# One state-space block on one core: moving the step-size series, its exponential and the taps within four passes

## What is computed

```python
proj = einsum('bld,pd->blp', hidden_states, in_proj_w)     # gate | x,B,C | dt
conv = conv_bias + sum_k pad[:, k:k+L, :] * conv_weight[:, k]   # 4 taps
xBC = silu(conv)
dt_p = softplus(dt + dt_bias)
dA = exp(dt_p * -exp(A_log))
# scan: state = state * dA + (dt_p * x) outer B ;  y_t = state . C
y = (ys + x * D) ; yn = y * rsqrt(mean(y*y) + EPS) * norm_weight * silu(gate)
out = einsum('bli,di->bld', yn, out_proj_w)
```

## Time and profile before

| | us |
|---|---|
| median of 3 runs (lowest, highest) | 1552.02 (1550.84, 1553.86) |
| the profiled execution, its own time | 1551.53 |
| its span | 1549.7 |
| PE busy | 1522.1 (98%) |
| DVE busy | 1109.2 (72%) |
| ACT busy | 753.7 (49%) |
| POOL busy | 657.8 (42%) |

### The profile page before, as it was taken

The page is one execution under the profiler, slowest core; times in us unless marked ns, Lnnn a source line. Parts: engine busy times, 40 slices in busy tenths (PEclk is TensorE's granted clock), DMA queues, the critical chain, the costliest instruction groups (busy, mean ns, idle before and its releaser), DMA issues. The chain is left out here.

```text
span 1549.7 us, 31996 instructions
## 1 busy us (share of the span) xinstructions
PE 1522.1 (98%) x12855; PEld 1244.9 (80%) x12855; DVE 1109.2 (72%) x1717; ACT 753.7 (49%) x1306; POOL 657.8 (42%) x687
## 2 busy tenths in 40 slices
PE   7999999999999999999999999999999999999997
PEld 6878888888888888888778888888888888888686
DVE  5977777776667767677787767777676767777566
ACT  4754445445454445445465444545454544544452
POOL 3553544435253544434335352535434352533406
PEclk9999999999999999999999999999999999999999
DMA  5220212122120212121014121102121121113212
GB/s 202 79 86 22 69 35 71 53 62 62 49 76 17 74 35 69 55 62 49 18 55 127 55 69 49 57 27 76 42 69 56 55 69 48 52 32 99 94 36 109
DMA packets 57843, 97.71 MB, mean 63 GB/s; under 512 B 9120, under 2 KB 17824, under 8 KB 57696
## 3 DMA queue, kind: packets, MB, share of 16 engines
q1 hardware_dynamic: 57696, 95.67, 20.2%
HBM read 86.73 MB, written 8.91 MB: 62 GB/s over the span
## 5 line engine op out<-in xcount | busy, mean ns | idle before, releaser
L461 PE MATMUL PS<-xh,wh 128*128 128x512 f32 x1280 | 518.7, 405 | 0.6 <-DVE xl L959 0.6
L1027 DVE SCALAR_TENSOR_TENSOR cb<-PS,P,cb 128x496 f32<-128x496 f32 (+2 forms) x576 | 412.5, 716 | 129.5 <-ACT cb L768 115.9
L461 PE MATMUL PS<-xh,wl 128*128 128x512 f32 x1280 | 501.1, 391 | 0.0
L461 PE MATMUL PS<-xl,wh 128*128 128x512 f32 x1280 | 500.4, 391 | 0.0
L1321 POOL TENSOR_TENSOR wl<-rw,wh 128x512 fp32r<-128x512 f32 x160 | 209.9, 1317 | 214.6 <-ACT wh L714 214.4
L1331 POOL TENSOR_TENSOR ysum<-yq 128x256 f32<-128x256 f32 x128 | 109.2, 853 | 442.3 <-ACT yq L808 441.9
L461 PEld LDWEIGHTS PS<-xh,wl 128*128 128x128 f32 x1280 | 240.5, 188 | 52.5
L461 PEld LDWEIGHTS PS<-xh,wh 128*128 128x128 f32 x1280 | 240.9, 188 | 51.3 <-issue 1.0
L461 PEld LDWEIGHTS PS<-xl,wh 128*128 128x128 f32 x1280 | 241.1, 188 | 45.3
L768 ACT ACTIVATE cb<-PS,P 128x512 f32<-128x512 f32 x192 | 148.3, 772 | 195.4 <-PE PS L461 195.4
L557 PE MATMUL PS<-oh,yh 128*128 128x512 f32 x512 | 200.7, 392 | 4.9 <-issue 3.3
(11 more groups left out here) (188 smaller groups left out, 1880.7 us busy)
## 6 DMA issues: line engine op xcount, KB each, us to landing
rw<-in_w_in SPq DMA_DIRECT2D x160, 256.0 KB, 2.8
ro<-in_w_out SPq DMA_DIRECT2D x64, 256.0 KB, 2.9
dab<-rates SPq DMA_DIRECT2D x128, 128.0 KB, 3.1
x2s<-acc SPq DMA_DIRECT2D x16, 256.0 KB, 3.1
out_x<-acc SPq DMA_DIRECT2D x16, 256.0 KB, 3.0
acc<-in_x SPq DMA_DIRECT2D x3, 1024.0 KB, 9.8
wh<-x2s SPq DMA_DIRECT2D x8, 256.0 KB, 3.8
wl<-x2s SPq DMA_DIRECT2D x8, 256.0 KB, 4.5
```

Of the source, the lines that this page charges most:

```text
L461: mm = e.matmul(PS[:, proj_bank(n, m), :], w[:, m, 128 * k:128 * k + 128], v[:, k, a:a + 512], start=(i == 0), stop=(i == 11))
L1027: e.scalar_tensor_tensor(out=cv[:, :, d:32], in0=pv[:, :, 0:32 - d], scalar=P[:, P_CW + 4 * c + 3 - d:P_CW + 4 * c + 4 - d], in1=cv[:, :, ...
```

## The change

The change moves instructions and adds none. In DVE's `stage`, the taps of pass 0 come first in their slot, ahead of the mix operands; the operands of tiles 4, 5 and 6 are written in slot 0 behind the taps, those of tile 7 in slot 2. The series of block 0 stays in slots 1 to 3 of pass 0, now behind taps and mixed parts. The series of blocks 1, 2 and 3 ran in slot 9 of one pass and slots 2 and 3 of the next; now all twelve operations run in slot 4 of the next pass (1, 16, 17), behind taps and mixed part. On ACT the exponential stands ahead of the evacuation, in slot 4 of pass 0 and in slot 5 of passes 1, 16 and 17, where it stood behind evacuation 4. POOL zeroes the rates in the same slots; in pass 0 it builds weights 1 ahead of the split of weight tile 3, and weights 3 in slot 4, behind the split of weight tile 8, where it did so in slot 3.

```diff
@@ scalar_program, stage(n)
+                    if n in TURNED and m == (5 if n else 4):
+                        rates_exp(TURNED[n])
                     evac(n, m)
-                    if n in TURNED and m == 4:
-                        rates_exp(TURNED[n])
@@ vector_program, stage(n)
-                    if n == 0 and m == 1:
+                    if n == 0 and m < 6:
+                        taps(0, m)
+                    if n == 0 and m == 0:
                         mix_operands(4)
                         mix_operands(5)
+                        mix_operands(6)
+                    if n == 0 and m == 2:
+                        mix_operands(7)
...
-                    if b is not None and m in (2, 4):
+                    if n and b is not None and m in (2, 4):
                         mix_operands(4 * b + 1 + m // 2)
...
-                    if n == 0 and 1 <= m <= 3:
-                        dt_series(0, 4 * m - 4, 4 * m)
-                    if b is not None and m == 9:
-                        dt_series(b, 0, 4)
-                    if n - 1 in BLOCK_AT and m in (2, 3):
-                        dt_series(BLOCK_AT[n - 1], *((4, 8), (8, 12))[m - 2])
-                    if m < 6:
+                    if n and m < 6:
                         taps(n, m)
                     if n % 2 == 0 and m >= 6:
                         split_o_lo(n // 2, m - 6)
                     if b is not None and 2 <= m <= 5:
                         mixed_lo(4 * b + m - 2)
+                    if n == 0 and 1 <= m <= 3:
+                        dt_series(0, 4 * m - 4, 4 * m)
+                    if n - 1 in BLOCK_AT and m == 4:
+                        dt_series(BLOCK_AT[n - 1], 0, 12)
@@ gpsimd_program, stage(n)
-                    if m == 4 and n in TURNED:
+                    if n in TURNED and m == (5 if n else 4):
                         first_rates(TURNED[n])
...
-                    if n == 0 and m in (2, 3):
-                        mixing_weights(m)
+                    if n == 0 and m in (2, 4):
+                        mixing_weights(1 + m // 2)
@@ gpsimd_program, ahead of the loop
-            for T in range(4):
+            for T in range(3):
                 split_w_lo(0, T)
             mixing_weights(1)
+            split_w_lo(0, 3)
```

## The result

The changed kernel took 1553.99 us (median of 20 runs, 1552.17 to 1555.97), the kernel before, timed beside it, 1551.49 (20 runs, 1550.75 to 1553.86). The ratio is 1.0015, 95% interval 1.0009 to 1.0022: 2.5 us slower, where the prediction had 1.1 us faster (1.6 by its sum). The time lies within the range of the prediction and within the 0.2% that it called no change, but the sign is the other one and the interval excludes no change, so the sum is wrong by about 4 us.

A forecast was written before the change was run, and what follows sets the result against it. TensorE is busy almost throughout, so only its waits count. Terms 1.5 - 2.3 + 4.9 - 2.5 make 1.6 faster: from the profiled 1551.53 to 1549.9, with the median 0.49 above, 1550.4 us; range 1545.0 to 1556.0.

The forecast's parts named there:

- Pass 0, the lead: Pass 0: tile 1's taps follow evacuation 1, the Gram products start at 32.4, and PE leads by 6.9 us.
- Pass 0, what is late next: Pass 0: series ends at 45.6, x's turn starts at 55.2 after PE waits 3.3; 1.5 us gained net.
- That chain: Pass 0, from series' end to x's turn: exponential, evacuation, splits, weights 3, ACT's gate evacuation, copy and SiLU; 9.6 us.
- the old fall behind the wait of 4.70: Pass 0 before the change: lower clock on six matmuls after the Gram products' wait for tile 1's SiLU, 1.2 us.
- Passes 1 and 17, the gain: Slots 2 and 3 lose the series, y of tile 2 comes 2.7 us earlier, and the gap of 1.63 goes.
- The 1.63: PE's wait in pass 1 before the output product at 91.94, repeated in pass 17 with 1.64; forecast to go.
- Passes 1 and 17, the loss: Series in slot 4 delays the rates' load and y products: 2.3 us lost in pass 1, 2.5 in pass 17.
- Pass 16: PE's waits of 0.68 and 2.27 for mixed tiles go, with 1.65 of clock: 4.9 us gained, no new wait.
- The end: From pass 18 on PE is full, so the summed shift, 1.6 us faster, reaches the end.
- Rival 4: Passes 1 and 17: the rates' wait is long enough for the clock to fall; 6.7 us slower, 1558.7, chance 0.12.
- Table loads: ACT: the exponential's table load runs ahead of the wait for its data and costs nothing.
- Rival 5: Table loads cost more: started only after the series, 1554.2, chance 0.05; with the page's drain, 1553.2, chance 0.03.

The follow-up runs named there:

- experiment 2: Kernel before with only the later blocks' part of the change (series in slot 4, exponential in slot 5), first pass as before: 1554.50 us, ratio 1.0016.
- Experiment 10: Changed kernel with mixing weights 2 and 3 of pass 0 placed later, their scratch and inputs in other buffers: 1550.01 us, ratio to before 0.9994.
- 13: Kernel before with only block 3's series moved to slot 4 of pass 17, its exponential to slot 5: 1554.53 us, ratio 1.0016.
- experiment 14: Kernel before with only block 1's series moved to slot 4 of pass 1, its exponential to slot 5: 1555.26 us, ratio 1.0021.
- experiment 4: Changed kernel with the rates' loads in passes 1 and 17 directly behind the stores, ahead of weight tile 8: 1549.30 us, ratio to before 0.9984.

## Why the prediction was wrong, by its own steps

The chains were right and the sum was not. In timed runs, by the prediction's terms: pass 0 +1.5 forecast, +0.9 measured; block 1 -2.3, measured -3.7; block 2 +4.9, measured +3.8; block 3 -2.5, measured -3.0. All four missed to the same side, but each forecast lies within the interval of its own experiment. Clear misses are the whole change and experiment 2, forecast 0.1 faster and measured 1.1 to 3.7 slower.

The traces put the loss elsewhere than the medians: pass 0 +0.6 for 1.5; pass 1 -2.1 in the change for 2.3, so its term was right in size; pass 16 +3.4 or +5.0 for 4.9; pass 17 -4.1 for 2.5; and from pass 18 on -0.7 to -1.2 in six of eight executions with block 3 changed, for nothing. With some 4.2 for pass 16 and 1.0 for the end these make 2.4 slower, and 2.5 were measured.

- **Pass 0, the lead.** Taps first, Gram products at 32.10 (forecast 32.4), operands in time: right.
- **Pass 0, what is late next.** The step that failed is "four operations 2.9 ..., to 34.5", taken as uncovered. The prediction put mixing weights 2 beside the second four operations alone; they began at 34.54, beside operation 3, and a weight split stood beside operation 2. The first four took 6.1 (31.25 to 37.39), and the second four, which ran free, ended at 43.4 instead of 40.8. So the series ends at 48.2 instead of 45.6, x's turn starts at 57.6 instead of 55.2, and of the lead of 3.0 there, 0.6 is left to pay the clock loss of 1.5. That chain (9.4 for 9.6) and that clock loss were right. Experiment 10, with weights 2 and 3 moved, ends the series at 45.5 and is 4.0 faster. The 1.2 taken for the old fall behind the wait of 4.70 came from the one trace where this fall was short.
- **Passes 1 and 17, the gain.** The 1.63 is gone: right.
- **Passes 1 and 17, the loss.** The chain through SyncE's queue was right to the microsecond: rates' load 4.67 later (forecast 4.1, and TensorE came 0.9 later into the pass), y products +2.9 with that 0.9 in it. The step that failed is "each under 1.7, so no clock loss is taken". In both profiled executions of the change the clock fell in pass 1, behind a wait of 1.66 and 1.69, where the wait for the rates hides it (experiment 2 loses as much there without a fall), and in pass 17 behind the two later waits (1.34 and 0.93), where it costs: 4.1 instead of 2.5. That the sums of tile 3 would "start just where they did before" was short too: they wait 1.66. The series is 6.6 long by its own terms, where the prediction writes 6.4, and took 7.1 (94.21 to 101.29).
- **Pass 16.** Both gaps went and nothing new came: right, and the 4.99 of the trace is the 4.9 forecast. What was mis-sized is its worth in a median: 1.65 of it was a fall of the clock that two of four traces of this part as before don't have. Measured 3.8.
- **The end.** "From pass 18 on PE is full, so the shift reaches the end" failed too: one more fall of the clock in the last 30 us, 0.7 to 1.2, for a cause that stays open.
- **Rival 4** named the right mechanism on the right side, with the wrong deciding point (a length of wait between 1.64 and 2.27). There is none: 1.63 and 1.64 without a fall, 1.66 with and without, 2.27 with and without, and in pass 0 1.54 with and without. Its 6.7 was too much, since in pass 1 the wait for the rates hides the fall.
- **Table loads** ran ahead of the waits as forecast: the load stands at 93.08 and its exponential at 101.33, 0.04 after the series' end. Rival 5 falls. With the Trainium skill's page (ScalarE: Activation LUTs, "What ACT_TABLE_LOAD costs") the load's 1283 ns agree once more (Silu's load at 102.43, its activation at 103.73), and its drain of about 1380 ns again shows in no row.

## What to carry to other kernels

Work that "collides with nothing" must be laid beside the other engine's timeline operation by operation, at its new times: a shift of a few us put two short operations beside long ones of GpSimd. Ask for each wait that is removed how often its cost really occurs, by the same stretch in several executions; a stretch with a clock's fall in the one trace at hand overstates the gain. Count the stretch from its own start, not from the kernel's: the start alone varied by 2 us here. And a transfer behind another in one queue is worth more than the arithmetic around it: one moved line (experiment 4) turned a loss into a gain.

## What the runs showed of the hardware

- A VectorE operation with operands in SBUF alone ended 0.27 and 0.29 us after the GpSimd operation that ran when it was due, even where that meant 2.49 instead of 0.42; the taps, which read PSUM, kept their 0.7 beside the same GpSimd work.
- TensorE's clock after like waits: 1.66 us, a fall behind it in pass 1 of both executions of the change and none in pass 17 of the same executions, while it fell there in experiments 2 and 13; none in pass 1 of experiment 14; 2.27 us, a fall in two executions of four; 1.54 in pass 0, a fall in three of six. Behind the 4.70 and the 2.9 of pass 0 there is one in every trace. A fall in passes 1, 16 and 17 was up to 3.4 us of matmuls at 1.2 GHz and cost about 1.6. With matmuls put into the waits of passes 1 and 17 none was seen in two executions.
- A table load is carried out while the activation behind it still waits for its data, 8 us ahead here.
